# Local attention layers: a new order on all engines, values one iteration later, the mask as eight small matmuls

## The reference

```python
def local_attention(q, k, v):          # w = 32; each window sees itself and the one before
    ...
    mask = (it < jb) | (it > jb + w) | (jb == -1)
    sim = jnp.einsum('bhwie,bhwje->bhwij', bq, bk2) * QK_SCALE
    sim = jnp.where(mask, -jnp.finfo(sim.dtype).max, sim)
    attn = jax.nn.softmax(sim, -1)
    out = jnp.einsum('bhwij,bhwje->bhwie', attn, bv2)
...
def attn_layer(x, Wqkv, qs, ksc, Wo):
    q, k, v = jnp.split(x @ Wqkv, 3, -1)
    q = l2norm(q) * qs                 # and k; both are then rotated by position
    ...
    return local_attention(q, k, v) @ Wo
...
def ffn_layer(x, g, bln, W1, b1, W2, b2):
    mu = x.mean(-1, keepdims=True)
    var = ((x - mu) ** 2).mean(-1, keepdims=True)
    xn = (x - mu) / jnp.sqrt(var + 1e-05) * g + bln
    a, gate = jnp.split(xn @ W1 + b1, 2, -1)
    return a * jax.nn.gelu(gate, approximate=False) @ W2 + b2
...
for i in range(DEPTH):                 # DEPTH = 6
    x = attn_layer(shift_tokens(x), ...) + x
    x = ffn_layer(shift_tokens(x), ...) + x
```

## Time and profile before

| | |
|---|---|
| median of 3 runs | 6171.74 us (6170.45 to 6173.91) |
| the profiled execution | 6156.9 us, span 6155.0 us |
| mean granted TensorE clock | 0.929 of full |
| busy: PE, DVE, ACT, POOL | 5313.4, 4157.3, 2766.2, 2397.5 us |
| costliest lines | 1360 POOL 984.8 us, 1103 PE 1242.7, 1400 DVE 936.2 |

### The profile page before, as it was taken

The page is one execution under the profiler, slowest core; times in us unless marked ns, Lnnn a source line. Parts: engine busy times, 40 slices in busy tenths (PEclk is TensorE's granted clock), DMA queues, the critical chain, the costliest instruction groups (busy, mean ns, idle before and its releaser), DMA issues. The chain is left out here.

```text
span 6155.0 us, 169853 instructions
## 1 busy us (share of the span) xinstructions
PE 5313.4 (86%) x71376; PEld 3397.7 (55%) x71376; DVE 4157.3 (68%) x6338; ACT 2766.2 (45%) x5037; POOL 2397.5 (39%) x2148
## 2 busy tenths in 40 slices
PE   5878778786868778999999999999999999999997
PEld 3857667585848564444454545554444445545554
DVE  6565665566565647777777777777777777777774
ACT  4232232414132315555555555555555555555554
POOL 2232222222222315444444444444444444444442
PEclk8888888788878879999999999999999999999999
DMA  0000000000000002222222222222222222222222
GB/s 20 3 2 4 1 4 1 4 1 4 1 4 1 3 29 62 55 59 71 64 57 60 66 71 59 60 64 71 60 60 54 74 65 60 60 69 61 57 59 57
DMA packets 255842, 252.15 MB, mean 41 GB/s; under 512 B 29680, under 2 KB 248688, under 8 KB 254704
## 3 DMA queue, kind: packets, MB, share of 16 engines
q1 hardware_dynamic: 255088, 241.29, 15.5%
HBM read 29.90 MB, written 4.19 MB: 6 GB/s over the span
## 5 line engine op out<-in xcount | busy, mean ns | idle before, releaser
L1360 POOL TENSOR_TENSOR turn<-prod 128x512 f32<-128x512 f32 x768 | 984.8, 1282 | 1936.7 <-DVE prod L1400 970.1
L1103 PE MATMUL banks<-w2s,xs 128*128 128x512 f32 x2304 | 1242.7, 622 | 98.4 <-DVE xs L1432 90.5
L1400 DVE TENSOR_TENSOR prod<-banks,tabs 128x1024 f32<-128x1024 f32 x768 | 936.2, 1219 | 113.9 <-ACT sq L1247 113.5
L1247 ACT ACTIVATE sq<-banks 128x512 f32<-128x512 f32 x768 | 459.3, 598 | 954.0 <-PE banks L1103 949.9
L1369 POOL TENSOR_TENSOR turn<-turn,rs 128x512 f32<-128x512 f32 x768 | 833.9, 1107 | 87.9 <-ACT rs L1264 84.1
L660 POOL TENSOR_TENSOR ao<-at,msk 128x512 f32<-128x512 f32 x288 | 388.4, 1360 | 1044.7 <-PE banks L412 563.8
L1133 PEld LDWEIGHTS banks<-msk,turn 128*128 128x128 f32 x3072 | 325.4, 141 | 573.5 <-issue 564.5
L1436 DVE TENSOR_REDUCE mx<-banks 128x8 f32<-128x512 f32 x384 | 265.7, 692 | 378.1 <-PE banks L1119 376.0
L1411 DVE TENSOR_REDUCE ss<-sq 128x8 f32<-128x512 f32 x768 | 519.4, 676 | 1.5
L854 DVE TENSOR_TENSOR tr<-tr,banks 128x512 f32<-128x512 f32 x240 | 165.4, 689 | 510.1 <-PE banks L436 508.8
L614 ACT ACTIVATE p<-banks 128x512 f32<-128x512 f32 x288 | 172.0, 597 | 722.1 <-PE banks L412 722.1
(11 more groups left out here) (202 smaller groups left out, 9827.0 us busy)
## 6 DMA issues: line engine op xcount, KB each, us to landing
v<-v_tok SPq DMA_DIRECT2D x1152, 132.0 KB
v<-v_tok SPq DMA_DIRECT2D x384, 66.0 KB
v<-v SPq DMA_DIRECT2D x188, 132.0 KB, 2.6
w2s<-in_weights SPq DMA_DIRECT2D x10, 768.0 KB, 4.6
tabs<-in_rot SPq DMA_DIRECT2D x40, 128.0 KB, 2.7
w2s<-in_weights SPq DMA_DIRECT2D x1, 2713.5 KB, 11.0
w2s<-in_weights SPq DMA_DIRECT2D x10, 256.0 KB, 3.0
xin<-in_x SPq DMA_DIRECT2D x8, 256.0 KB, 2.9
```

What stands on the lines that cost most here:

```text
L1103: pe.matmul(a_bank(use), xs[:, t % 2, b * P:(b + 1) * P], w[:, at:at + 512], start=True, stop=True).then_inc(a_done, 1)
L1247: a.activation(sq[:, r % 2, :], a_bank(use), ACT.Square).then_inc(sq_done, 1)
L1360: gp.tensor_tensor(turn[:, r % ROTS, :, :].rearrange(halves, s=2), prod[:, r % 2, 0, :, :].rearrange(halves, s=2), prod[:, r % 2, 1, :, :] ...
L1400: v.tensor_tensor(prod[:, r % 2, :, :, :], a_bank(use).rearrange("p (h d) -> p h d", h=HU).unsqueeze(1) .to_broadcast([P, 2, HU, DH]), tab ...
```

## The change

- TensorE: the mask becomes eight matmuls, one for each of the eight 64x32 places that the scores use; `idb` is cut to the 32 columns and 64 rows of a place, and `kmask` holds two tables in place of eight. The order within an iteration is new. `values` and `turn_att` work for iteration `g - 1`, `output` for `g - 2`.
- ScalarE and VectorE follow in a new order; the GELU table is loaded ahead by hand in iteration 4; the inverse norms come last. `normalise` now works for `g - 1` and stands between the first sums and the second rotate. The residual of the FFN moves from iteration 0 to iteration 1, `shifted_in` from iteration 1 to iteration 7, for the tile after the next.
- POOL's and SP's order stay.

```diff
@@ -977,14 +978,13 @@
                 a_use["x", g, 2] = len(a_use)
             for name in ffn_products(g):
                 a_use["c", g // 8 - 1, name] = len(a_use)
+            if order:
+                t_use[order[0]] = len(t_use)
+                t_use[order[1]] = len(t_use)
+            if 0 <= g < NIT:
+                t_use["p", g] = len(t_use)
             if 0 <= g - 1 < NIT:
                 t_use["att", g - 1] = len(t_use)
-            if order:
-                t_use[order[0]] = len(t_use)
-            if 0 <= g < NIT:
-                t_use["p", g] = len(t_use)
-            if order:
-                t_use[order[1]] = len(t_use)
 
         def item(g, n):
             U, i = (g + LEAD) // 4, (g + LEAD) % 4
...
@@ -1108,10 +1108,14 @@
                         pe.wait_ge(t_taken, t_use["q", U, 3] + 1)
                         if g:
                             pe.wait_ge(sub_done, g)
-                        for h in range(2):
-                            pe.matmul(blocks(sc[:, h, :]), idb[:],
-                                      kmask[:, t % NT:t % NT + 1, :].to_broadcast([P, NB, 2 * WIN]),
-                                      start=True, stop=False, skip_group_check=True)
+                        kind = min(t % NT, 1)
+                        for n in range(NW):
+                            for h in range(2):
+                                r = slice(h * DH, (h + 1) * DH)
+                                at = h * DH + min(n, 1) * WIN
+                                pe.matmul(blocks(sc[n * WIN:(n + 1) * WIN, h, :]), idb[r, at:at + WIN],
+                                          kmask[r, kind:kind + 1, :].to_broadcast([DH, NB, 2 * WIN]),
+                                          start=True, stop=False, skip_group_check=True)
                         for b in range(NB):
                             for n in range(NW):
                                 for h in range(2):
...
@@ -1213,24 +1217,24 @@
                         order = turns(g)
                         if attend:
                             scores(g)
+                        if 0 <= g - 2 < NIT:
+                            output(g - 2)
+                        if order:
+                            turn_heads(order[0])
                         if feed:
                             project(g, 0)
-                        if behind:
-                            turn_att(g - 1)
+                        if order:
+                            turn_heads(order[1])
                         if feed:
                             project(g, 1)
-                        if order:
-                            turn_heads(order[0])
                         if behind:
-                            output(g - 1)
+                            values(g - 1)
                         if attend:
                             turn_probs(g)
                         if feed:
                             project(g, 2)
-                        if order:
-                            turn_heads(order[1])
-                        if attend:
-                            values(g)
+                        if behind:
+                            turn_att(g - 1)
                         for name in ffn_products(g):
                             ffn(g // 8 - 1, name)
...
@@ -1326,24 +1330,26 @@
                     for g in range(FIRST, LAST):
                         feed, attend, behind = g + LEAD < NIT, 0 <= g < NIT, 0 <= g - 1 < NIT
                         order, U = turns(g), (g + LEAD) // 4
-                        if feed:
-                            square(g, 0)
-                        if behind:
-                            take_att(g - 1)
+                        if order:
+                            take_heads(order[0])
                         if attend:
                             exponents(g)
                         if feed:
+                            square(g, 0)
+                        if order:
+                            take_heads(order[1])
+                        if feed:
                             square(g, 1)
-                        if order:
-                            take_heads(order[0])
+                        if 8 <= g and g % 8 == 4:
+                            a.preload_act_table_set(GELU)
                         if attend:
                             take_probs(g)
+                        if feed:
+                            square(g, 2)
+                        if behind:
+                            take_att(g - 1)
                         if feed and g % 2:
                             inverse_norms(2 * U + (g + LEAD) % 4 // 2)
-                        if feed:
-                            square(g, 2)
-                        if order:
-                            take_heads(order[1])
                         if 8 <= g:
                             ffn(g // 8 - 1, g % 8)
...
@@ -1514,22 +1520,17 @@
                         if feed:
                             rotate(g, 0)
                             sums(g, 0)
-                        if 8 <= g and g % 8 == 4:
-                            ffn(g // 8 - 1, 4)
+                        if 8 <= g and g % 8 in (1, 4):
+                            ffn(g // 8 - 1, 0 if g % 8 == 1 else 4)
+                        if 0 <= g - 1 < NIT:
+                            normalise(g - 1)
                         if feed:
                             rotate(g, 1)
-                        if 8 <= g and g % 8 == 1:
+                            sums(g, 1)
+                        if 8 <= g and g % 8 in (1, 2, 5, 6):
                             ffn(g // 8 - 1, g % 8)
-                        if feed:
-                            sums(g, 1)
-                        if 8 <= g and g % 8 == 0:
-                            ffn(g // 8 - 1, 0)
-                        if attend:
-                            normalise(g)
-                        if 8 <= g and g % 8 in (2, 5, 6):
-                            ffn(g // 8 - 1, g % 8)
-                        if g % 8 == 1 and 0 <= g < NIT - 8:
-                            shifted_in(g // 8 + 1)
+                        if g % 8 == 7 and g // 8 + 2 < TILES:
+                            shifted_in(g // 8 + 2)
                         if g % 8 == 3 and 0 <= g // 8 - 1 < TILES - NT:
                             scale_table(g // 8 - 1)
             nc.all_engine_barrier(sems_to_clear=range(wq_loaded.num, xm_done.num + 1))
...
@@ -1591,11 +1592,11 @@
         s = 1 << n
         low = (i // (2 * s) == j // (2 * s)) & (i // s % 2 == 1) & (j // s % 2 == 0)
         m[:, M_OFF + n], m[:, M_OFF + LEVELS + n] = low, low.T
-    key = np.zeros((P, NT, 2 * WIN), np.float32)
+    key = np.zeros((P, 2, 2 * WIN), np.float32)
     r, k = (np.arange(P) % WIN)[:, None], np.arange(2 * WIN)[None, :]
     hidden = np.where(k < WIN, k < r, k - WIN > r)
     key[:] = np.where(hidden, MASKED, 0.0)[:, None, :]
-    key[0:WIN, 0, 0:WIN] = MASKED
+    key[np.arange(P) % DH < WIN, 0, 0:WIN] = MASKED
     half = np.arange(0, DH, 2, dtype=np.float32)
     inv_freq = (1.0 / 10000.0 ** (half / np.float32(DH))).astype(np.float32)
     pos = np.arange(L, dtype=np.float32)
```

More of the change, by code:

```diff
@@ L50 @@
 LN_EXP = "natural_log_exp_and_others"
+GELU = "gelu_and_others"
 LN_SHIFT = 20
@@ L928, in local_layers @@
         tabs = sb("tabs", [P, NT, 4, DH])
-        kmask = sb("kmask", [P, NT, 2 * WIN], BF16)
+        kmask = sb("kmask", [P, 2, 2 * WIN], BF16)
         idb = sb("idb", [P, P], BF16)
@@ L1003, in _ @@
             def _(sp):
-                sp.dma_start(sq[:, 0, :], key_mask).then_inc(w_init, 16)
+                sp.dma_start(sq[:, 0, 0:4 * WIN], key_mask).then_inc(w_init, 16)
                 sp.dma_start(tabs[:], rot).then_inc(w_init, 16)
@@ L1015, in _ @@
                 v.wait_ge(w_init, 48)
-                v.tensor_copy(kmask[:].rearrange("p t n -> p (t n)"), sq[:, 0, :]).then_inc(init_ready, 1)
+                v.tensor_copy(kmask[:].rearrange("p t n -> p (t n)"), sq[:, 0, 0:4 * WIN]).then_inc(init_ready, 1)
                 v.tensor_tensor(tabs[:].rearrange("p t i d -> p t (i d)"),
@@ L1609, in shape_constants @@
     tab = tab.reshape(NT, P, 4, DH).transpose(1, 0, 2, 3).astype(np.float32)
-    return m, key.reshape(P, NT * 2 * WIN), np.ascontiguousarray(tab)
+    return m, key.reshape(P, 4 * WIN), np.ascontiguousarray(tab)
 def laid_out(d):
```

## The result

| | before | after |
|---|---|---|
| median of 4 runs each | 6171.09 us | 6332.86 us |
| ratio, 95% interval | | 1.0267 [1.0254, 1.0280] |
| span of the profiled execution | 6155.0 us | 6331.6 us |
| mean granted TensorE clock | 0.929 | 0.928 |

The forecast was 122 us more; 162 were measured. Two views of the profile after give the balance: the mask's line with its first and last start, and the busy times of the engines in the stretch of the earlier trace rows.

What follows compares the result with a forecast made beforehand. TensorE was taken as the bound; 9.1 us of new waits less 5.4 old and 1.7 mask, plus 0.6 clock, gave 2.6 us per period, 122 us over 47 periods: 6294 us, own range 6245 to 6340, 8 in 10 6155 to 6380.

Steps and rivals of the forecast that it cites:

- mask, on TensorE: Start of each iteration: eight tiled mask matmuls cost 0.10 us, saving 0.21 per iteration, 1.7 per period.
- new waits: Waits the new order adds in iterations 0 to 6: 1.5 + 3.3 + 1.7 + 0.7 + 1.9 = 9.1 us per period.
- clock: TensorE's long gap in iteration 4 halves its clock: 1.4 us lost less the present 0.8, +0.6 per period.
- Scores and values apart: In TensorE's order, other blocks now separate values from scores: all 77.6 us of "issue" waits go, part of the 5.4.
- Place 1: Iterations 3, 5 and 6: the first FFN product waits 0.49 us for the second rotate to free its bank, 1.5 together.
- Place 2: Iteration 4: FFN normalisation ahead of `normalise` makes `att` wait 2.66 us, the gate's bank 0.67; together 3.3.
- Place 3: Iteration 7 to 0: `shifted_in`, 1.65 us, delays the next maximum, so `att` waits 1.7 us.
- POOL's share lies under it: Iteration 0: POOL's normalisation lets heads turn at 2.7 instead of 1.73 us, hidden under the 1.7 us `att` wait.
- The sign named as wrong: The forecast is wrong if `att` waits under 2 us in iteration 4, or not at all in 0 and 2.
- Place 4: Iteration 1: the residual, a carry and an add taken as 0.85 us, precedes `normalise`; `att` waits 0.7 us.
- Place 5: Iteration 2: `xf` copies delay the maximum, so `att` waits 1.3 us and the mean's bank 0.7; together 1.9.
- That rival: VectorE's extra work slides into its idle time before the first rotate: -2.4 us per period, 6059 us, chance 0.18.

Runs made afterwards that it cites:

- the reduction: Changed kernel with iteration 1's four-column carry on VectorE made by a one-element reduction instead of a copy: 6303 us, 1.0225 to the kernel before.
- the two fastest kernels: Changed kernel with VectorE's FFN work right behind the subtraction (and key copy), 6024 us; the same with heads also turned behind the projections, 5877 us.

## Why the prediction was right, and where its terms were off

Per period in us, by the prediction's terms:

| term | predicted | measured |
|---|---|---|
| old waits gone | -5.4 | -5.4 |
| mask, on TensorE | -1.7 | -1.2 |
| new waits | +9.1 | +10.1 |
| clock | +0.6 | near 0 |
| sum | +2.6 | +3.5 |

The forecast fell short by 40 us, 0.9 per period: the new waits were 1.0 above it and the mask 0.5 short, and the clock, 0.6 the other way, hid part of that. That it came so near is in part luck.

- *The mechanism* is shown: with VectorE's work taken out of places 2 to 5 and nothing else changed, the kernel is 309 us faster. With the old mask the period is 82.9 us, so the order alone cost 4.4 us per period, some 207 us, and the mask gave some 44 back.
- *The mask* was taken too large: 0.21 us per iteration, where 0.11 was measured. "The change from whole array to tiles is paid once either way" is what the traces show, but the sum didn't follow it. The old time to the first score held that change: with the old mask in the new order the second mask matmul starts 0.11 us after the first, and the first score 0.20 after the second. The 0.10 set against it held none; the change is now paid ahead of the mask, in the transposes' 0.56 instead of 0.46. The pace was right: the eight matmuls of 0.28 last 0.30 together, but the scores start 0.12 after the first (predicted 0.10). Eight times 0.11 is 0.9; the other 0.3 of the 1.2 is the clock, which in these two executions fell after 27 of 44 gaps in iteration 4 with the old mask and after 19 with the new.
- *Scores and values apart*: all "issue" waits went, as chosen.
- *Place 1*: 0.46 us in iterations 3, 5 and 6, predicted 0.49.
- *Place 2*: `att` 2.36 and the gate 0.47, predicted 2.66 and 0.67; the second heads wait 0.29 besides.
- *Place 3* had the wrong place and too small a size: 1.04 for POOL's normalisation and 1.35 for the copy `kx`, 2.4 in all, against 1.7 for `att`. The step "POOL's share lies under it" failed, since the first heads wait for POOL and the second then for the late maximum, one behind the other. And `shifted_in` was priced at 1.65 from the earlier trace rows, where POOL delayed one copy; here both wait for it, 1.12 and 1.16, and the maximum starts 2.34 after the first. The sign named as wrong ("none in 0") did appear for `att`: the wait sat earlier, at the heads.
- *Place 4*: 1.46, predicted 0.7. "A carry and an add" left POOL out: the carry waits 0.7 us for it, and with the reduction 0.74 remained.
- *Place 5*: of 88 waits for POOL half lie here, about 1.05, with 0.31 for `att` and 0.47 for the mean's bank: 1.8 together, predicted 1.9, but not in the pieces named: 1.3 for `att` and 0.7 for the bank. That the sum agrees is luck.
- *The clock*: 0.99 in the stretch, as before. It falls after 19 of 44 gaps in iteration 4, not in each period. The kernel before had 17 falls in as many periods, in iterations 1 and 2, and those went.
- *The rivals*: no "issue" waits came back, and the tiles did not run in turn. VectorE's work was not absorbed where it stands. That rival named the gap that the two fastest kernels use, and a reason why the changed order can't use it.

## What to carry to other kernels

When a late step of an engine's order is moved up, price everything that it now passes or stands behind, at the place where it will run: the same copies took 0.41 or 1.12 us, depending on whether POOL was running beside them. Put an engine's spare work into the gap where it waits for others, ahead of the work that others wait for. A faster instruction is worth what its neighbours leave of it: read from the instruction before it to the one after it, and try it in the order in which it will stand.

## What was not expected of the hardware

- VectorE's operations inside the SBUF wait for a running POOL operation: 0.41 to 1.12 us, 0.68 to 1.39, 0.55 to 1.15; a copy of 4 elements per partition 0.16 to 0.87. Its reductions and its products from the banks keep their length: 674 to 680 ns for 768 sums, 690 to 693 for 384 `att`.
- The transposes ahead of small tiles take 0.56 us, ahead of whole-array matmuls 0.46.
- The same gap of 1.94 us, with the same releaser, was followed by half the clock in 19 of 44 periods of one kernel and in 2 of 44 of another.
